# A graph network's edge stages: GpSimd issues the scatters of a finished batch before the gathers of the batch two ahead

## What is computed

```python
x = layernorm(x + gcn(relu(gcn(x, W1, b1)), W2, b2))        # two convolutions: CONV1, CONV2
x = layernorm(x + x @ root + bias + mean over relations r of sum over edges (x @ W[r])[src])   # MEAN
x = layernorm(x + sum over edges of softmax weight * (x @ W[type])[src])                       # scores, ATTEND
x = layernorm(x + relu(sum over edges of (x @ W[type])[src]))                                  # SUM
```

## Time and profile before

| what | value |
|---|---|
| three runs | 4040.19, 4043.31, 4044.37 us (median 4043.31) |
| profiled execution | span 4810.3 us; the page gives no other time of it |
| TensorE (PE) busy | 3060.5 us, 64% of the span |
| VectorE (DVE) busy | 2972.0 us, 62% |
| GpSimd (POOL) busy | 2636.3 us, 55%; 2559 instructions |
| ScalarE (ACT) busy | 1695.3 us, 35% |
| mean granted TensorE clock | 0.812 |

### The profile page before, as it was taken

How to read it: one execution, slowest core, us unless ns; L and a number is a source line. 1 busy time by engine, 2 the same in 40 slices (tenths; PEclk the granted TensorE clock), 3 DMA queues, 4 the chain that set the end, 5 groups by cost and what they waited for, 6 DMA issues and landing times. The chain is left out here.

```text
span 4810.3 us, 58978 instructions
## 1 busy us (share of the span) xinstructions
PE 3060.5 (64%) x10737; PEld 1722.6 (36%) x10737; DVE 2972.0 (62%) x8605; ACT 1695.3 (35%) x4812; POOL 2636.3 (55%) x2559
## 2 busy tenths in 40 slices
PE   3565454444444333334777675777769996999997
PEld 2343333333333333233323232444434332444443
DVE  6664445555555555556666572444459996888887
ACT  2555545544444444444333331111114443111111
POOL 3555555555554555554666765666623444666665
PEclk9777776676766666766888886888879998999999
DMA  2554334333333333333112221222212222112111
GB/s 83 166 169 138 129 129 128 103 109 110 110 120 96 98 105 109 102 110 103 46 51 57 59 54 58 73 73 71 75 49 67 83 83 67 39 46 51 51 51 38
DMA packets 271071, 415.85 MB, mean 86 GB/s; under 512 B 65268, under 2 KB 128709, under 8 KB 271002
## 3 DMA queue, kind: packets, MB, share of 16 engines
q1 hardware_dynamic: 189466, 280.05, 18.5%
q0 software_dynamic: 81536, 135.07, 10.1%
HBM read 215.50 MB, written 218.72 MB: 90 GB/s over the span
## 5 line engine op out<-in xcount | busy, mean ns | idle before, releaser
L1137 PE MATMUL bank<-sum_masked,sum_w 128*128 128x512 f32 x1568 | 691.0, 594 | 1.4 <-issue 1.4
L1408 POOL DMA_INDIRECT at_rows<-t_x,at_gi x392 | 395.4, 1009 | 242.6 <-issue 141.3
L1137 PE MATMUL bank<-mean_masked,mean_w 128*128 128x512 f32 x784 | 420.3, 667 | 154.5 <-DVE mean_masked L1214 104.4
L1214 DVE SCALAR_TENSOR_TENSOR sum_masked<-sum_typ,sum_col 128x512 f32<-128x512 bf16 x784 | 488.3, 685 | 32.8 <-ACT sum_col L1067 30.9
L1465 PE MATMUL bank<-at_masked,at_ww 128*128 128x512 f32 x784 | 413.8, 677 | 114.2 <-DVE at_masked L1504 93.9
L1504 DVE SCALAR_TENSOR_TENSOR at_masked<-at_typ,at_col 128x512 f32<-128x512 bf16 x392 | 245.3, 689 | 318.2 <-ACT at_col L1442 183.9
L1137 PEld LDWEIGHTS bank<-sum_masked,sum_w 128*128 128x128 f32 x1568 | 291.2, 191 | 332.2 <-issue 274.8
L1137 PE MATMUL bank<-att_masked,att_w 128*128 128x512 f32 x784 | 379.6, 612 | 9.1 <-DVE att_masked L1214 7.2
L1033 POOL DMA_INDIRECT t_x<-att_new,att_si x196 | 194.2, 991 | 315.8 <-ACT att_new L1095 268.8
L1025 POOL DMA_INDIRECT c_rows<-t_g,c_gi x196 | 188.3, 961 | 290.3 <-ACT c_gi L1048 211.7
L1025 POOL DMA_INDIRECT sum_rows<-t_x,sum_gi x196 | 229.3, 1170 | 203.1 <-ACT sum_gi L1048 158.0
(11 more groups left out here) (263 smaller groups left out, 6869.7 us busy)
## 6 DMA issues: line engine op xcount, KB each, us to landing
t_x<-c_dense_x SPq DMA_DIRECT2D x196, 256.0 KB
pf_xc<-x_dram SPq DMA_DIRECT2D x98, 256.0 KB
t_g<-pf_g SPq DMA_DIRECT2D x98, 256.0 KB
t_x<-pf_x SPq DMA_DIRECT2D x98, 256.0 KB
out_dram<-c_dense_x SPq DMA_DIRECT2D x98, 256.0 KB
t_x_even<-pf_x SPq DMA_DIRECT2D x49, 256.0 KB
c_dense_x<-t_x SPq DMA_DIRECT2D x49, 256.0 KB
c_same<-p_same SPq DMA_DIRECT2D x98, 128.0 KB
```

Of the source, the lines that this page charges most:

```text
L1137: pe.matmul(H[q][:, :], w[:, r, :], masked[:, r % MASKS, :], start=(r == 0), stop=(r == n_rel - 1))\
L1214: v.scalar_tensor_tensor(out=masked[:, r % MASKS, :], in0=typ[:, q, :], scalar=float(r), in1=col[:, q, :], op0=ALU.is_equal, op1=ALU.mult) ...
L1408: pool.indirect_dma_start(rows[:, q, side, j, :], None, m.tables["X2"], bass.IndirectOffsetOnAxis(ap=gi[:, q, side, j:j + 1], axis=0))\
```

## The change

In GpSimd's body the two groups change places, with their waits: first the hold for `new_ready` and the four scatters of batch b-lag, then the holds for `idx_ready` and the free slot and the four gathers of batch b+2. Slots, semaphores, counts and all other engines' programs stay. The first bodies of a stage (b < lag) have no scatters, the last ones no gathers, and are the same as before; so is all of ATTEND.

```diff
         @block.gpsimd
         def _(pool):
             def body(b, q):
+                s = b - lag
+                qs = (q + lag) % 2
+                if runs(s, 0, LAST):
+                    hold(pool, new_ready, s + 1)
+                    for j in range(BT):
+                        pool.indirect_dma_start(out, bass.IndirectOffsetOnAxis(ap=si[:, qs, j:j + 1], axis=0),
+                                                new[:, qs, j, :], None, bounds_check=NP - 1, oob_is_err=False)\
+                            .then_inc(scattered[qs], 16)
                 s = b + 2
                 if kind != ATTEND and runs(s, 0, LAST):
                     hold(pool, idx_ready, s + 1)
...
                                                 bass.IndirectOffsetOnAxis(ap=gi[:, q, j:j + 1], axis=0))\
                             .then_inc(gathered[q], 16)
-                s = b - lag
-                qs = (q + lag) % 2
-                if runs(s, 0, LAST):
-                    hold(pool, new_ready, s + 1)
-                    for j in range(BT):
-                        pool.indirect_dma_start(out, bass.IndirectOffsetOnAxis(ap=si[:, qs, j:j + 1], axis=0),
-                                                new[:, qs, j, :], None, bounds_check=NP - 1, oob_is_err=False)\
-                            .then_inc(scattered[qs], 16)
             go(pool, body)
```

## The result

| | median of the runs | range | runs |
|---|---|---|---|
| before | 4041.75 us | 4036.00 to 4044.37 | 4 |
| after | 4105.72 us | 4102.73 to 4107.77 | 4 |

The ratio is 1.016 [1.0145, 1.0174]: the change costs 64 us. The forecast was 4064 us with a range to 4100: slower was right, and the size was too small by a factor of three (+21 forecast, +64 measured).

What follows compares the result with a forecast made beforehand. GpSimd was taken to be saturated in CONV1, CONV2 and MEAN, about 10.3 us a batch, TensorE to bound SUM. Shift 13.2 + CONV1 loop 7 + MEAN 1 = +21 us on 4043: 4064 us, range 4038 to 4100 (likeliest case 4051 to 4082).

Steps and rivals of the forecast that it cites:

- the stops: Halts of ScalarE and GpSimd in the profiled execution (span 4810 us, 767 over the timed median), taken as absent from timed runs.
- The shift: Starts of CONV1, CONV2, MEAN: gathers begin later behind one scatter group, +5.6, +2.6, +5.0 us, sum +13.2 us.
- The loop in CONV1: CONV1 gathers, landing, L1060, `c_new`, scatters, next gathers: 20.3 or 21.3 us against GpSimd's 20.6 for two batches; +7 us.
- its cover: CONV1: two GpSimd bodies, 20.6 us, hide the loop; formerly 4 to 5 us to spare, now used up.
- last gather to L1060 at most 2.7: CONV1 loop term: from the last gather's issue to ScalarE's scaling L1060, at most 2.7 us.
- I take the middle, +0.35: CONV1 loop excess between nothing and +0.7 us per pair, taken as +0.35 x 21 pairs = +7 us.
- MEAN's loop covered: MEAN: two GpSimd batches, 21.7 us, leave 9.2 for ScalarE's part; covered, +1 us for jitter, 5 at the upper end.
- CONV2's loop covered: CONV2: the loop runs over three bodies (31 us), so it costs 0.
- SUM at 0 with some us less slack: SUM: later gathers still lie behind TensorE's products, 16 us of slack; 0 us, 6 us at the upper end.
- Ring and ScalarE add up: Rival: gathers behind scatters land 3.2 us after issue, CONV1's TensorE products always slow; +50, 4093 us; chance 0.12.
- Real stops: Rival: the profile's stops are in timed runs too, ScalarE 3.6 us late per CONV1 pair; 4132 us; chance 0.10.
- No change: Rival: GpSimd isn't saturated in timed runs, so shift vanishes and later landing is covered; 4043 within 8 us; chance 0.20.
- Faster: Rival: in MEAN scatters land earlier and ScalarE's wait ahead of `mean_si` goes; -11, 4032 us; chance 0.08.

Runs made afterwards that it cites:

- the second profile: The changed kernel run and profiled again, no further edit: 4096.25 us against 4034.38 for the kernel before, 1.0158.
- experiments 6 and 7: Both on the changed kernel: 6, CONV1 scatters batch b-5 instead of b-4, 4037.98 us; 7, CONV1's `c_new` made before the dense second and third steps, 4057.96 us.
- the second profile of before: The kernel before profiled again, no edit: 4030.74 us, profiled span 4028.9 us.
- Experiments 8 and 9: Quarter of dense stores in CONV1, CONV2: changed order 4320.82 us; loads too: 5019.38, again 4314.92; order of before, both cuts: 5073.30, again 4271.74.

## Why the prediction was off

**What bounds the kernel: right.** The compared runs are without the stops, and GpSimd is saturated in CONV1 (two batches in 20.9 us without a gap, 20.6 forecast). That the stops belong to the profiled execution was wrong: in one group of runs the timed executions had them as well. Where they come from is open.

**The shift: right.** Forecast 5.6, 2.6 and 5.0 us later gathers in CONV1, CONV2 and MEAN; found 4.9, 2.6 and 5.9 (4.2 in MEAN in the second profile). In the time MEAN's shows as +4.0 and goes with a batch more of lag; CONV2's 2.6 can't be told from nothing in the total (-1.0, between -6 and +2).

**The loop in CONV1: the mechanism right, its size wrong by a factor of seven.** This is the step that failed. The forecast had the loop complete, step by step as the runs show it, and that its cover is used up; experiments 6 and 7 show it from two sides (a lag more takes 58 of CONV1's 60 us away, 1.3 to 1.6 us less in ScalarE's part takes away 37). Its terms, against the rows of the changed kernel:

| term | forecast | measured |
|---|---|---|
| first to last gather | 3.8 | 3.95 |
| last gather to L1060 | at most 2.7 | 4.39 |
| L1060 to the end of `c_new` | 7.8 or 8.8 | 8.79 |
| to the scatter | 0.8 | 0.89 |
| scatters | 5.2 | 5.24 |
| sum | 20.3 or 21.3 | 23.26 |
| two batches of GpSimd | 20.6 | 20.9 |

The mis-sized term is "last gather to L1060 at most 2.7". It was read from the first batches of CONV1, where SyncE has issued a dense load (794.60) but no dense store yet (the first at 799.64), and called "at most", where it is near the least that the steady stretch has. The rows of MEAN said 3.2, and the second profile of before has 2.5 to 4.6 in CONV1's steady stretch. The profile that the forecast had couldn't say so: with its stops, L1060 waits for the rows in 1 of the batches 8 to 42. In the changed kernel the bounding batch always has the late landing, 4.4 us. The rows show it beside SyncE's dense transfers: its last gather is issued at 887.79 between the dense load (887.45) and the stores (888.15 to 889.18). The other batch's last gather is out at 898.37 and SyncE's dense transfers come only at 901.22: at most 2.7 us. Experiments 8 and 9 show about 1.1 of the 1.7 us to be this traffic; the other 0.6 stay open.

The second error is in the same step: "I take the middle, +0.35". The two values of ScalarE's term, 7.8 and 8.8, were treated as a coin thrown in each pair. In this loop the bounding batch had 8.8 every time, with L1166 at the granted clock of 0.50 after TensorE had been idle for 9 us. By the forecast's upper value alone the loop would have cost 15 us; with 4.4 for the landing it is 23.0 - 20.6, x 21 = 50 us, and the sum 13 + 50 + 1 = +64, the time measured. That it fits to the microsecond is partly luck: of the 13 us of shift some 9 show in the time, and the loop's two sides were each 0.3 us short.

**The rest.** MEAN's loop covered: right, its batches stay at GpSimd's 11 us. CONV2's loop covered: right. SUM at 0 with some us less slack: right (13.8 us left). That L1060 would be ready in the kernel before and wait for its rows only in the changed one was wrong: without the stops it waits in 28 of the 35 batches 8 to 42 before, too. ATTEND unchanged: right, within run-to-run spread (420.0 us, then 416.9 when the changed kernel ran again; before 416.0).

**The rivals.** *Ring and ScalarE add up* came nearer to the time (4093), by luck: its parts were 25 us in CONV1's loop, 12 in MEAN's and 13 of shift, where 52, none and about 9 were found. Its ScalarE half was right; its ring half fell: with lag 5 the gathers stand behind scatters in every batch and are used as before, 3.2 / 3.3 us after the last issue against 3.1 / 3.3, and in MEAN the mean is 2.7 us before and 2.8 after, so the row of 3.2 was a late one. The rule of the Trainium skill that was weighed for it (DMA: Bandwidth & Descriptors, "Two DMAs through the same engine are not ordered") thus had no visible price at these sizes; the same sentence of it says that descriptors start in order but are pipelined, which the forecast left out. What did delay gathers came from another issuer. The same page, "Queues, rings and completion order", says that a DMA engine takes turns between the queues that have work for it; the rows with 4.4 us beside SyncE's transfers and 2.7 without agree with that, but give no proof of it. *Real stops*: fell for the runs that were compared; where the stops were real, the change with its dense traffic in full wasn't run, and with a quarter of it the changed order was the faster one. *No change*: fell in CONV1 and MEAN; CONV2 and SUM didn't change, but not for its reason, since GpSimd is saturated in CONV2 (two batches in 20.6 us) and TensorE bounds SUM. *Faster*: fell; in the runs without the stops no stage got shorter beyond the spread.

## What to carry to other kernels

When one group of work is put ahead of another on an in-order queue, write down the loop that now closes through both and compare it with the period of the engine that covers it; below it the move is free but for the shift, above it the whole excess is paid in every turn. Take each term of that loop, latencies above all, from the loaded steady stretch and at its slowest, not from the pipeline's start or as a mean: the loop here settled on one phase, and it was the slow one. If the only profile has stops that the timed runs don't have, take another before reading such terms. If the order is wanted all the same, one batch more of lag bought the cover back here (58 us of CONV1's 60), and in every stage it left no difference to the kernel before.

## What the runs showed of the hardware

Four indirect gathers of 128 rows of 512 bytes were in the rows' tile at most 2.7 us after the last one's issue when none of SyncE's dense transfers was issued beside it, 3.8 with its loads and a quarter of its stores beside it, 3.2 with a quarter of both, and 4.4 with all of them. No engine's busy time shows this; only the time from issue to first use does. In the kernel before the same spread, 2.5 to 4.6 us, is there and costs nothing.

TensorE's product L1166 took 2.08 us at a granted clock of 0.50, after 9.04 us without work, and 1.12 us at 1.00, after 2.00 us without work, in the other batch of the pair. The loop that made TensorE idle so had some 0.85 us of its 23.3 from this.

A group of runs in which every kernel took 4.8 to 5.1 ms in place of 4.0 to 4.3, timed executions as well as profiled ones, wasn't expected. There the changed order with a quarter of the dense traffic was 54 us faster than the other order, where it was 43 us slower otherwise. By the two profiles some 13 us of the 54 are in CONV1, 11 in CONV2 and 25 in MEAN, a stage whose traffic wasn't cut. With that cut, which order is better depends on whether the stops are there; for the changed kernel in full it wasn't measured, and the cause of the stops stays open.
